# A fused two-layer transformer kernel: the first head group's row maxima of layer 1 in two halves, and row scores paced by columns

## The reference, cut to what matters

```python
q = (x @ W_query).reshape(b, n, NUM_HEADS, HEAD_DIM).transpose(0, 2, 1, 3)
k = (x @ W_key).reshape(b, n, NUM_HEADS, HEAD_DIM).transpose(0, 2, 1, 3)
v = (x @ W_value).reshape(b, n, NUM_HEADS, HEAD_DIM).transpose(0, 2, 1, 3)
scores = jnp.einsum('bhqd,bhkd->bhqk', q, k)
scores = jnp.where(causal, -jnp.inf, scores)
attn = jax.nn.softmax(scores / jnp.sqrt(jnp.float32(HEAD_DIM)), axis=-1)
ctx = jnp.einsum('bhqk,bhkd->bhqd', attn, v)
return ctx.transpose(0, 2, 1, 3).reshape(b, n, D_OUT) @ W_out + b_out
```

## Time and profile before

| | us |
|---|---|
| median of 3 runs | 1362.34 (1362.08 to 1362.48) |
| the profiled execution | 1362.7 |
| its span | 1361.0 |
| attention of layer 1, from the first row item to the last score step | 764.8 to 1059 |

### The profile page before, as it was taken

How to read it: one execution, slowest core, us unless ns; L and a number is a source line. 1 busy time by engine, 2 the same in 40 slices (tenths; PEclk the granted TensorE clock), 3 DMA queues, 4 the chain that set the end, 5 groups by cost and what they waited for, 6 DMA issues and landing times. The chain is left out here.

```text
span 1361.0 us, 18268 instructions
## 1 busy us (share of the span) xinstructions
PE 1243.6 (91%) x5944; PEld 859.5 (63%) x5944; DVE 812.6 (60%) x1732; ACT 589.7 (43%) x1091; POOL 470.8 (35%) x335
## 2 busy tenths in 40 slices
PE   6999999999999999999998968889997478999887
PEld 6866878888887788888885512223322247778665
DVE  6467754444444344444456767777775556878565
ACT  2322633333333333333334425766777153433553
POOL 3101445555555555555563221111111033312000
PEclk9999899999999999999999969999999788999899
DMA  4100253333332643333421350232200301110001
GB/s 152 41 20 1 82 147 109 108 108 108 108 108 54 160 111 108 108 108 108 108 70 47 128 159 22 77 79 70 70 17 17 87 0 47 34 48 24 1 15 47
DMA packets 49308, 102.67 MB, mean 75 GB/s; under 512 B 8660, under 2 KB 21716, under 8 KB 49244
## 3 DMA queue, kind: packets, MB, share of 16 engines
q1 hardware_dynamic: 49244, 101.87, 26.6%
HBM read 88.52 MB, written 8.93 MB: 72 GB/s over the span
## 5 line engine op out<-in xcount | busy, mean ns | idle before, releaser
L473 DVE TENSOR_TENSOR q_t<-q_t,ps 128x512 f32<-128x512 f32 x132 | 90.8, 688 | 230.3 <-ACT q_t L416 227.7
L1554 DVE CUSTOM_DVE_ANT_0 masked<-ps,causal 128x128 f32<-128x128 f32 (+7 forms) x256 | 184.4, 755 | 55.9 <-PE ps L1375 55.1
L529 POOL TENSOR_TENSOR wqkv<-q_t,v_tok 128x512 f32<-128x512 f32 x132 | 198.0, 1516 | 25.9 <-DVE q_t L473 15.2
L519 POOL TENSOR_TENSOR d_w_lo<-raw,d_w_hi 128x768 fp32r<-128x768 f32 x66 | 122.7, 1860 | 242.8 <-ACT d_w_hi L389 242.8
L465 DVE TENSOR_TENSOR wqkv_lo<-wqkv,wqkv_hi 128x512 fp32r<-128x512 f32 x132 | 155.0, 1174 | 67.9 <-ACT wqkv_hi L395 67.9
L311 PE MATMUL ps<-h_hi,d_w_hi 128*128 128x512 f32 x528 | 167.2, 397 | 1.9 <-POOL d_w_lo L519 1.0
L311 PE MATMUL ps<-h_hi,d_w_lo 128*128 128x512 f32 x528 | 166.0, 395 | 0.0
L311 PE MATMUL ps<-h_lo,d_w_hi 128*128 128x512 f32 x528 | 166.0, 395 | 0.0
L1534 ACT ACTIVATE xn<-ps 128x512 f32<-128x512 f32 (+3 forms) x256 | 117.3, 512 | 58.1 <-PE ps L1395 56.3
L389 ACT CAST d_w_hi<-raw 128x768 fp32r<-128x768 f32 x66 | 55.0, 833 | 195.1 <-PE ps L324 193.5
L311 PEld LDWEIGHTS ps<-h_hi,d_w_hi 128*128 128x128 f32 x528 | 98.9, 189 | 25.8 <-POOL d_w_lo L519 1.9
(11 more groups left out here) (252 smaller groups left out, 2119.1 us busy)
## 6 DMA issues: line engine op xcount, KB each, us to landing
v_tok<-router_weights_t SPq DMA_DIRECT2D x132, 256.0 KB, 3.8
raw<-in_moe SPq DMA_DIRECT2D x66, 384.0 KB, 4.3
qk<-qk_parts SPq DMA_DIRECT2D x72, 128.0 KB, 2.7
qk_parts<-parts SPq DMA_DIRECT2D x16, 384.0 KB, 2.7
raw<-in_mlp SPq DMA_DIRECT2D x16, 384.0 KB, 3.1
h_t<-qk_parts SPq DMA_DIRECT2D x24, 128.0 KB, 2.8
x_tok<-in_x SPq DMA_DIRECT2D x4, 512.0 KB, 8.2
h_hi<-raw SPq DMA_DIRECT2D x32, 64.0 KB, 2.3
```

The source lines that it names most:

```text
L473: nc.vector.tensor_tensor(prod[:, s % 3, :], sg[:, s % 3, :], ps[:, 2 * (s % 2) + 1, :], ALU.mult).then_inc(s_t, 1)
L519: nc.gpsimd.tensor_tensor(w_lo[:, slot, :], raw[:, slot, :], w_hi[:, slot, :].bitcast(F32), ALU.subtract).then_inc(s_wlo, 1)
L529: nc.gpsimd.tensor_tensor(inter[:, s % 3, :], prod[:, s % 3, :], wbc[:, s // 2, (s % 2) * GW:(s % 2 + 1) * GW], ALU.mult).then_inc(s_int, 1)
L1554: nc.vector.tensor_tensor_reduce(masked[:, at % 2, 0:k], ps[:, bank:bank + 2, :].rearrange("p a n -> p (a n)")[:, 0:k], causal[:, SEQ - k: ...
```

## The change

It does four things.

1. Group 0's maxima come in two halves. The entries are sorted: first the 16 items of 1 to 4 blocks of the four heads, then one item 5, then a new entry `FIRST`, then the other long items. `FIRST` and the old R of group 0 each handle 16 maxima: a `minus_max` chain on VectorE, a transpose of 48 instead of 96 columns, a copy of 48 rows to `mrow`. Score tiles 0 to 3 of group 0 need only the first half, tile 4 waits for the second.
2. Each half is moved by four transfers of 3 x 4 x 128 values, one a head, instead of one for all. `first_rows()` stands in SP's order before store 10; `rows(0)` stands behind store 15, ahead of group 2's loads.
3. `ahead` falls from 36 to 20: the 16 short items, one item 5, `FIRST` and two more items.
4. `due` goes by columns: an item counts its width and two blocks more, a step likewise, and entries are due in proportion. The leads at the end of a group are 2, 5, 8 and 10 entries past its R; R of the last group falls due with the last tile of group 6. The remainders stand one entry earlier.

```diff
-                EARLY, LATE_ROWS, LEAD = 2, 3, 9
+                EARLY, LATE_ROWS = 2, 3
+                LEAD = (2, 5, 8, 10)
+                ROWS, FIRST, HALF = HQ * TB, HQ * TB + 1, 3 * HQ * TB // 2
+                short = [n for n in range(HQ * TB) if n % TB < GW // P]
+                long = [n for n in range(HQ * TB) if n % TB >= GW // P]
+                entries = [(0, n) for n in short] + [(0, long[0]), (0, FIRST)] + [(0, n) for n in long[1:]]
...
-                due = [min(len(entries), ahead + (at * 3 + min(h, 2) + 1) * (HQ * TB + 1) // (3 * NTI)
-                           + min(LEAD, at * LEAD // NTI)) for at in range(NV * NTI) for h in range(HQ)]
+                def target(v, steps):
+                    goal = lambda u: filled[min(len(entries), place[u, ROWS] + LEAD[min(u, 3)])]
+                    if v == 0 and steps <= half_way:
+                        a, b, at, of = filled[ahead], goal(0), spent[steps], spent[half_way]
+                    elif v == 0:
+                        a, b, at, of = goal(0), goal(1), spent[steps] - spent[half_way], spent[-1] - spent[half_way]
+                    else:
+                        a, b, at, of = goal(v), goal(min(v + 1, NV - 1)), spent[steps], spent[-1]
+                    return a + (b - a) * at // of
...
+                        def half_rows(at, done):
+                            for h in range(HQ):
+                                sp.dma_start(qs[0][KR:KM, h, at:at + GW],
+                                             mrow[h * HALF // HQ:(h + 1) * HALF // HQ, :]).then_inc(done, 16)
...
+                            if j == 10:
+                                first_rows()
                             if j == 12:
                                 load_qk(sp, 1)
...
+                        rows(0)
                         sp.wait_ge(s_proj, NJ)
                         load_qk(sp, 2)
...
-                        rows(0)
...
-                            if n == 0 and h == 0:
-                                pe.wait_ge(s_rows, 16 * (v + 1))
+                            if n == 0 and h == 0 and v == 0:
+                                pe.wait_ge(s_first, 64)
+                            if n == (0 if v else 4) and h == 0:
+                                pe.wait_ge(s_rows, 16 * (v + 4))
```

More of the change, by code:

```diff
@@ L3 @@
+import itertools
 from contextlib import ExitStack
@@ L1233, in build, with columns @@
                             entries.append((v, n))
-                        if v and n == (LATE_ROWS if v > 1 else 0):
-                            entries.append((v - 1, HQ * TB))
+                        if n == (LATE_ROWS if v > 1 else 0):
+                            entries.append((v - 1, ROWS))
                 place = {e: n for n, e in enumerate(entries)}
-                ahead = place[0, HQ * TB] + 1 + EARLY
-                due = [min(len(entries), ahead + (at * 3 + min(h, 2) + 1) * (HQ * TB + 1) // (3 * NTI)
-                           + min(LEAD, at * LEAD // NTI)) for at in range(NV * NTI) for h in range(HQ)]
+                ahead = place[0, FIRST] + 1 + EARLY
+                def columns(n):
+                    return (n % TB + 1) * P + 2 * P if n < ROWS else 2 * P
+                filled = [0] + list(itertools.accumulate(columns(n) for _, n in entries))
+                spent = [0] + list(itertools.accumulate(
+                    (4 * g + 4 - max(4 * g, j)) * P + 2 * P for g, j in tiles for h in range(HQ - 1)))
+                half_way = 4 * (HQ - 1)
+                def target(v, steps):
[7 more added lines that the diff above has]
+                    return a + (b - a) * at // of
+                due = [sum(c <= target(v, n * (HQ - 1) + min(h, HQ - 2) + 1) for c in filled[1:])
+                       for v in range(NV) for n in range(NTI) for h in range(HQ)]
                 p_pre = xn[:, :, :].rearrange("p (r a) d -> p r (a d)", a=2)
@@ L1261, in build @@
                 s_cst = [sem("f_cst0"), sem("f_cst1")]
+                s_first = sem("f_first_rows")
                 s_bank = [0, 6]
@@ L1557, in maximum, with minus_max @@
                                 accum_out=hmax[:, v % 2, n:n + 1]).then_inc(s_mx, 1)
-                        def minus_max(v):
-                            m = hmax[:, v % 2, :]
-                            part = [mparts[:, n * HQ * TB:(n + 1) * HQ * TB] for n in range(3)]
+                        def minus_max(v, kind, last):
+                            cols = chunk_columns(v, kind)
+                            blocks = slice(0, TB) if v else slice(0, TB // 2) if kind == FIRST else slice(TB // 2, TB)
+                            by_head = lambda ap: ap.rearrange("p (h i) -> p h i", h=HQ)
+                            m = by_head(hmax[:, v % 2, :])[:, :, blocks]
+                            part = mparts[:, cols]
+                            if v:
+                                part = [part.rearrange("p (n h i) -> p n h i", n=3, h=HQ)[:, n] for n in range(3)]
+                            else:
+                                part = [part.rearrange("p (h n i) -> p h n i", n=3, h=HQ)[:, :, n] for n in range(3)]
+                            rest_of = by_head(hrest[:, 0:(cols.stop - cols.start) // 3])
```

57 lines of the change are left out of this document (37 added, 20 removed).

## The result

The changed kernel takes 1389.5 us (median of 4 runs, 1383.1 to 1391.9), before 1362.4: a ratio of 1.018, with an interval of 1.015 to 1.021. The forecast was 1377, with a range of 1367 to 1385. The direction was right and the loss was nearly twice the 15 us foretold. The profiled execution took 1391.3, with a span of 1389.6.

What follows compares the result with a forecast made beforehand. The prediction took TensorE's sequence as the bound, held up by items waiting for VectorE. Terms +5.0 to group 1's start, +9.6 and +1.8 sum to +16.4, or +13.2 at the full clock; taken as +15: 1377 us, range 1367 to 1385.

Steps and rivals of the forecast that it cites:

- the sum at the full clock: Whole kernel: the terms added with TensorE's clock never at half speed, a loss of 13.2 us.
- The front: Up to the first score step: it goes at 793.5 instead of 806.07, a gain of 12.6 us.
- Tiles 0 to 3: Group 0, first step to tile 4: 24.2 us (21.0 at the full clock) against 15.1, 9.1 us lost.
- half speed up to 804: Start of group 0: TensorE at half rate after the idle hole, moving tile 4 from 814.5 to 817.7.
- Tiles 4 to 11: Rest of group 0: more VectorE work, stepped to 33.8 us against 25.4, 8.4 us lost.
- the clock falls again in the row wait: Rival, wait at 813 to 817: tiles 4 and 5 at half speed, +2, kernel 1380 to 1384; 12%.
- The term of 9.6: Groups 1 to 5: the new item order loses 2.4 + 3.3 + 3.9 = 9.6 us.
- the 14% rival: Groups 1 to 5 cost only VectorE's added work, 1.1 + 1.4; kernel 1368 to 1372, or 1363; 14%.
- the tile of 4.7: Groups 3 to 5, tile 8,12,3: item 3 waits behind item 8 and the chain, stepped to 4.7 us.
- Group 6: The end: R falls due in tile 11, so the group takes 32.4 against 30.6, 1.8 us lost.

Runs made afterwards that it cites:

- e3: The changed kernel plus 154 TensorE products whose results are overwritten, placed where TensorE would wait: 1376.2 us, ratio 1.0086 to the kernel before.
- e1: The changed kernel with entries due evenly by number again from group 1 on, as in the kernel before: 1375.4 us, ratio 1.0078.
- e4: The changed kernel with the first half's four row transfers behind stores 10 and 11 on SP instead of ahead: 1386.4 us, ratio 1.0148.
- e7: The changed kernel with the old pace from group 1 on, and overwritten products added where TensorE would wait: 1365.7 us, ratio 1.0007.
- e2: The kernel before with only `due` by columns from group 1 on; front and group 0 are the old ones: 1381.1 us, ratio 1.0138.

## Why the prediction was off, point by point

The order of work was priced well: the sum at the full clock was +13.2, and e3's stage is +10.5. What failed is the price of the clock. Behind tile 3 of group 0 the sum has every tile at the full clock, and there the changed kernel lost 11.6 us against e3, 6.3 in tiles 4 to 11 and 5.3 in groups 1 to 5.

**The front: right.** Forecast 28.7 us after the first row item, measured 27.1 here and 28.8 in e1 and e3. The same instructions up to this step took 27.1 in one execution and 28.8 in another, so the miss of 1.6 says nothing. The store behind the four row transfers was what was waited for, and e4, which takes them out of its way, starts 3.9 earlier.

**Tiles 0 to 3: the right sum, in part by luck.** Forecast 24.2 from first step to tile 4, measured 24.2. The forecast had half speed up to 804, some ten us, as in the old kernel's slow spell. Measured, the clock was 0.50 through all 24.2 us and beyond. Two misses cancel: at the full clock these tiles were stepped at 21.0 and took 19.8 in e3, and the slow spell was priced at 3.2 and cost 4.4. The wait for the second half ended in:

```profile
813.87 0.27 PE L1416 MATMUL ps<-cbf,mparts 128*48 128x128 bf16 x1 [1.79 <-DVE mparts L1639]
...
814.42 3.06 SPq L1334 DMA_DIRECT2D qk<-mrow  x4
...
818.61 0.61 PE L1448 MATMUL ps<-qk 99*128 99x512 bf16 x1 [2.60 <-DMA qk<-mrow]
```

From the first of the four issues to the step it is 4.2, forecast 3 x 0.64 + 2.97 = 4.9; the first issue came 20.0 us after the first step, forecast 19.4, which makes up for it. Four issues took 3.12 and 3.06 us, the single one before 0.85. That is 2.2 to 2.3 more each time, where the prediction reckoned 1.9; no run tried the halves with one transfer each.

**Tiles 4 to 11: the first failed step.** "Stepped: 3.95, 4.45, 5.6, ... = 33.8" was made at the full clock. It is what e3 and e7 show to the tenth, and the changed kernel took 40.1. The prediction had this as a rival, "the clock falls again in the row wait", at 12% and +2: the mechanism was named, but it was given two tiles at the half rate. Measured it is 6.3 in these tiles. The clock hadn't come back before the row wait, stayed at the lower level for the first 7.1 us of these tiles, and fell twice more. Windows of the changed kernel:

```profile
818.60:825.70 7.10, 7.09 (x25) 2.04 (x25) 4.04 (x11) 2.99 (x5) 0.00 (x0) 0.50 0.57 171
825.70:829.10 3.40, 2.33 (x17) 0.67 (x15) 3.23 (x11) 1.36 (x3) 0.00 (x0) 1.00 0.69 188
829.10:839.40 10.30, 9.44 (x37) 2.42 (x29) 6.04 (x17) 4.39 (x8) 0.00 (x0) 0.50 0.00 0
839.40:846.20 6.80, 5.09 (x27) 1.32 (x25) 5.91 (x17) 2.99 (x5) 0.00 (x0) 1.00 0.00 1
846.20:849.60 3.40, 3.40 (x14) 0.84 (x14) 1.14 (x5) 1.09 (x2) 0.64 (x1) 0.50 0.00 0
```

**Groups 1 to 5: the second failed step.** The term of 9.6 put the clock's part at nothing. The order cost +9.9 in e3 (166.3 against 156.4), as forecast. But the changed kernel lost 15.2 and e2, with the pace alone, 14.2 in the same groups. The pace wasn't neutral, as the 14% rival had it, but worse than the forecast: the tile of 4.7 (e3 4.75) was 5.74 in group 4 of the changed kernel, the difference behind its waits. I had found those waits, with their lengths, and not asked what they do to the clock.

**Group 6: a small miss.** Its last tile took 6.80 (forecast 6.7), but tiles 0 to 10 took 23.9 and not 25.7, so the group cost 0.1 and not 1.8.

**The range.** With both terms at e3's clock the stage is +10.5, in the changed kernel +24.8: some 14 us hang on the clock. A range to 1385 took in one fall of it, not a repeated one.

The Trainium skill (TensorE: Matmul & The Clock Gate, A second HAM failure mode: psum-queue depth-cycling) tells of a kernel whose engine idles briefly between groups of products, so that its clock swings between the two rates. The rows of this case agree: in groups 1 to 5 of the changed kernel no wait of an item is over 1.2 us, and the clock is 0.90 to 0.95 in four of them. The prediction had used the page for the long wait ahead of tile 4 alone.

## What to carry to other kernels

Step a new order through at the full clock, then go back over each place where the engine waits twice in a short stretch, and price the work behind it at the half rate too, for the upper end of the range. Where a reordering moves waits together, keeping TensorE busy with products that nobody reads tells in one run how much of a loss is order and how much is clock. And look for the part of a change that only moves an issue on a queue: here that was worth 0.3% by itself, and the whole cost 1.8%.

## What the runs showed of the hardware

Waits of about one microsecond, far shorter than the hole ahead of the first step, can take the clock down; with products in them (e3) it stayed at 1.00. Waits of row items for VectorE in groups 1 to 5, before (846.5 to 1003.0) and in the changed kernel (858.7 to 1030.3), engine, line and releaser, then us in total, times, longest:

```profile
PE ps L1375 <- DVE hmax L1554: 14.4, 35, 0.8
```

```profile
PE ps L1426 <- DVE hmax L1611: 21.7, 35, 1.2
```

They are as many, but half as long again in all and at the longest. Before, the clock was 1.00 in all five groups; in the changed kernel it was 0.90 to 0.95 in four. A single long wait needn't do it: before, one of 1.21 us at the end of group 0 and one of 2.09 ahead of the last R left the clock at 1.00.

And the same waits don't do it each time. e4 has the changed kernel's order from group 1 on. In tile 7 of group 2 both wait 0.54, 0.70 and 0.83 us for VectorE. The last wait and the AV behind it, in the changed kernel and in e4:

```profile
915.80 0.34 PE L1426 MATMUL ps<-qk 96*128 96x384 bf16 x1 [0.83 <-DVE hmax L1611]
...
916.28 1.07 PE L1464 MATMUL ps<-rzb,v_ones 128*32 128x512 f32 x8
```

```profile
911.59 0.50 PE L1425 MATMUL ps<-qk 96*128 96x384 bf16 x1 [0.83 <-DVE hmax L1610]
...
912.45 1.94 PE L1463 MATMUL ps<-rzb,v_ones 128*32 128x512 f32 x8
```

The clock of the tile is 1.00 in one and 0.76 in the other, and group 2 takes 34.3 and 36.7. So a stepped order gives the places where the clock may fall, and not the times that it does. How long and how close waits must be is open; no run varied that by itself.

Adding work to TensorE made the kernel faster: 154 products in e3, for 13 us less. And in stretches that are the same in all kernels, the time from group 7's first step to the end differed by up to 10 us from trace to trace with the clock there; no experiment asked why.
